# Inverse square roots of a four-layer decoder moved from VectorE's Newton steps to GpSimd powers

## The reference, cut to what matters

```python
def _layernorm(x, axis=-1, eps=1e-05):
    m = jnp.mean(x, axis=axis, keepdims=True)
    v = jnp.var(x, axis=axis, keepdims=True)
    return (x - m) / jnp.sqrt(v + eps)
...
x = x + _L0_attn_ref(_layernorm(x, axis=-1), ...)
x = x + _L0_xattn_ref(_layernorm(x, axis=-1), ...)
...
```

```python
def _l2norm(x):
    return x * jax.lax.rsqrt(jnp.sum(x * x, -1, keepdims=True) + EPS)
```

## Time and profile before

| what | us |
|---|---|
| runs, median (lowest to highest) | 4525.57 (4521.23 to 4525.77) |
| profiled execution, span from first to last instruction | 4502.3 |
| median less the span | 23.3 |
| PE busy | 3949.4 (88%) |
| DVE busy | 2458.5 (55%) |
| ACT busy | 1538.8 (34%) |
| POOL busy | 829.5 (18%) |

### The profile page before, as it was taken

The page is one execution under the profiler, slowest core; times in us unless marked ns, Lnnn a source line. Parts: engine busy times, 40 slices in busy tenths (PEclk is TensorE's granted clock), DMA queues, the critical chain, the costliest instruction groups (busy, mean ns, idle before and its releaser), DMA issues. The chain is left out here.

```text
span 4502.3 us, 98249 instructions
## 1 busy us (share of the span) xinstructions
PE 3949.4 (88%) x39512; PEld 2449.6 (54%) x39512; DVE 2458.5 (55%) x6058; ACT 1538.8 (34%) x3480; POOL 829.5 (18%) x1464
## 2 busy tenths in 40 slices
PE   6998798898799879889879987988987998798898
PEld 4884344465588334446558833444655883344465
DVE  6674534554676453455466745345546765534554
ACT  4452222441454222243144422224314442222431
POOL 2430001130243010112024301011202430101220
PEclk9999999999999999999999999999998999999999
DMA  2001000000000100000000010000000001000000
GB/s 84 3 3 59 8 12 19 24 37 27 27 3 3 59 20 1 19 24 37 27 27 3 3 59 20 1 19 24 37 27 27 3 9 52 20 6 13 24 37 29
DMA packets 11013, 105.17 MB, mean 23 GB/s; under 512 B 1148, under 2 KB 5552, under 8 KB 6192
## 3 DMA queue, kind: packets, MB, share of 16 engines
q1 hardware_dynamic: 10544, 98.69, 5.7%
HBM read 97.64 MB, written 1.05 MB: 22 GB/s over the span
## 5 line engine op out<-in xcount | busy, mean ns | idle before, releaser
L88 PE MATMUL psum<-ident_bf 128*128 128x512 bf16 x2308 | 606.1, 400 | 196.1 <-DVE l_attn_peak L892 58.0
L88 PEld LDWEIGHTS psum<-ident_bf 128*128 128x128 bf16 x2308 | 220.5, 103 | 498.6 <-issue 141.9
L3251 DVE TENSOR_TENSOR l_attn_xx<-l_attn_xx,psum 128x256 f32<-128x256 f32 x512 | 204.4, 418 | 207.4 <-PE psum L2854 195.8
L3016 ACT ACTIVATE l_attn_ax<-psum 128x128 f32<-128x128 f32 (+1 forms) x768 | 185.3, 279 | 361.4 <-PE psum L2835 245.9
L482 DVE TENSOR_TENSOR l_ffn_hidden<-l_ffn_silu,psum 128x512 f32<-128x512 f32 (+2 forms) x176 | 120.9, 687 | 309.4 <-ACT l_ffn_silu L421 309.4
L421 ACT ACTIVATE l_ffn_silu<-psum 128x512 f32<-128x512 f32 (+1 forms) x208 | 124.2, 597 | 460.4 <-PE psum L390 406.8
L94 PEld LDWEIGHTS psum<-streamed_weights,l_ffn_hidden 128*128 128x128 f32 (+1 forms) x1664 | 214.8, 191 | 118.2 <-issue 101.0
L2850 PE MATMUL psum<-l_attn_ax,l_attn_xx 64*64 64x64 f32 x5120 | 267.8, 224 | 0.0
L2854 PE MATMUL psum<-l_attn_xx,l_attn_ax 64*64 64x64 f32 x5120 | 260.5, 221 | 0.0
L3140 POOL TENSOR_TENSOR l_attn_part<-l_attn_ab,streamed_weights 128x128 f32<-128x128 f32 x640 | 246.3, 417 | 39.4 <-PE psum L2835 20.3
L892 DVE TENSOR_REDUCE l_attn_peak<-psum 128x4 f32<-128x2048 f32 (+3 forms) x128 | 185.6, 1487 | 100.1 <-PE psum L789 100.0
(11 more groups left out here) (536 smaller groups left out, 8035.6 us busy)
## 6 DMA issues: line engine op xcount, KB each, us to landing
streamed_weights<-pack_l_ffn SPq DMA_DIRECT2D x4, 5284.0 KB, 16.2
streamed_weights<-pack_l_ffn SPq DMA_DIRECT2D x4, 3972.0 KB, 13.0
streamed_weights<-pack_l_attn SPq DMA_DIRECT2D x5, 2848.5 KB, 9.6
streamed_weights<-pack_l_xattn SPq DMA_DIRECT2D x4, 2496.0 KB, 8.6
streamed_weights<-pack_l_ffn SPq DMA_DIRECT2D x4, 2192.0 KB, 8.4
streamed_weights<-pack_l_xattn SPq DMA_DIRECT2D x4, 2048.0 KB, 8.2
streamed_weights<-pack_l_ffn SPq DMA_DIRECT2D x4, 1923.0 KB, 7.4
streamed_weights<-pack_l_attn SPq DMA_DIRECT2D x4, 1107.5 KB, 4.9
```

Source lines behind the costliest of these rows:

```text
L88: pe.matmul(self.bank(bank), self.ident_bf[:, :], self.ident_bf[:, :].unsqueeze(1).to_broadcast([P, NT, P]), start=True, stop=True)
L3016: act.activation(ax[b, p, :, :], m.psum[b, p, 0:P].rearrange("p (i t) -> p i t", i=2), ACT.Copy).then_inc(ax_ready, 1)
L3251: dve.tensor_tensor(both, both, m.psum[:, p, P:384], ALU.subtract).then_inc(x_less, 1)
```

## The change

`newton_rsqrt` goes from three of its callers. In its place VectorE's epsilon instruction signals GpSimd, GpSimd raises the variances to the power -0.5 (a TENSOR_TENSOR with `ALU.pow` against a column of -0.5 that is set once), and VectorE waits for that before it uses the roots. In the first layer VectorE now goes on to the next convolution chunk and takes the roots up one chunk later. The six warm-up matmuls in each norm that waited for the Newton chain go, and so do the last two groups (seven and four) in the head norm. The other two callers of `newton_rsqrt` stay as they are.

```diff
+        self.minus_half = self.sb("minus_half", [P, 1])
...
+    def root(self, pool, use):
+
+        pool.wait_ge(self.var_ready, use + 1)
+        pool.tensor_tensor(self.rstd[:, :], self.var[:, :], self.m.minus_half[:, :].to_broadcast([P, NT]),
+                           ALU.pow).then_inc(self.rstd_ready, 1)
+
     def statistics(self, dve, chain, src, eps):
...
-        chain.link(dve.tensor_scalar(self.var[:, :], self.mv[:, :, 1], eps, None, ALU.add))
-        newton_rsqrt(dve, chain, self.var[:, :], self.rstd[:, :], self.tmp[:, :])
+        dve.tensor_scalar(self.var[:, :], self.mv[:, :, 1], eps, None, ALU.add).then_inc(self.var_ready, 1)
...
     def tensor(self, pe):
         m = self.m
         m.warm(pe, 9, 2)
-        pe.wait_ge(self.chain, self.base + bool(self.add) + 9)
-        m.warm(pe, 6, 2)
...
     def gpsimd(self, pool):
...
         if self.keep:
             pool.tensor_tensor(m.x[:, :, :], m.x[:, :, :], m.xn[:, :, :], ALU.add).then_inc(self.kept, 1)
+        self.root(pool, self.use)
         if self.bias is not None:
...
     def vector(self, dve):
...
+        dve.wait_ge(self.rstd_ready, self.use + 1)
         for t in range(NT):
             dve.tensor_scalar(m.xn[:, t, :], self.src[:, t, :], self.mv[:, t, 0:1], self.rstd[:, t:t + 1], ALU.subtract,
                               ALU.mult).then_inc(self.xn_ready, 1)
...
(stage_l2_attn)
                 m.norm.gpsimd(pool)
+                pool.wait_ge(var_ready, 1)
+                pool.tensor_tensor(std[:, :, :], var[:, :, :],
+                                   m.minus_half[:, :].unsqueeze(2).to_broadcast([P, 2, NT * H]),
+                                   ALU.pow).then_inc(std_ready, 1)
...
-                for link in (4, 6, 11):
+                for link in (4, 6):
                     pe.wait_ge(chain_sem, link)
                     m.warm(pe, 7, 5)
-                pe.wait_ge(chain_sem, 17)
-                m.warm(pe, 4, 5)
...
-                chain.link(dve.tensor_scalar(var[:, :, :], var[:, :, :], 1.0 / HD, 1e-5, ALU.mult, ALU.add))
-                newton_rsqrt(dve, chain, var[:, :, :], std[:, :, :], tmp[:, :, :])
+                dve.tensor_scalar(var[:, :, :], var[:, :, :], 1.0 / HD, 1e-5, ALU.mult,
+                                  ALU.add).then_inc(var_ready, 1)
+                dve.wait_ge(std_ready, 1)
...
(stage_l0_attn)
                     pool.tensor_tensor(sq[:, i % 2, :], a, a, ALU.mult).then_inc(sq_ready, 1)
+                pool.wait_ge(norm2_ready, 1)
+                pool.tensor_tensor(rs[:, :, :], norm2[:, :, :], m.minus_half[:, :].unsqueeze(2).to_broadcast([P, NT, HV]),
+                                   ALU.pow).then_inc(root_ready, 1)
...
                     if n == NEWTON:
                         dve.wait_ge(sq_psum, 2 * F)
-                        newton_rsqrt(dve, chain, norm2[:, :, :], rs[:, :, :], rs_tmp[:, :, :])
+                        dve.tensor_scalar(norm2[:, :, :], m.psum[:, 6, 0:HV * NT].rearrange("p (t h) -> p t h", h=HV),
+                                          1e-6, None, ALU.add).then_inc(norm2_ready, 1)
+                    if n == NEWTON + 1:
+                        dve.wait_ge(root_ready, 1)
                         dve.tensor_scalar(rs[:, :, 0:2 * F], rs[:, :, 0:2 * F], W ** -0.5, None,
                                           ALU.mult).then_inc(rs_ready, 1)
```

More of the change, by code:

```diff
@@ L133, in __init__ @@
         self.rstd = m.sb("norm_rstd", [P, NT])
-        self.tmp = m.sb("norm_tmp", [P, NT])
         sem = m.pass_sem
         self.chain = sem("norm_chain")
+        self.var_ready = sem("norm_var_ready")
+        self.rstd_ready = sem("norm_rstd_ready")
         self.kept = sem("norm_kept")
@@ L172, in _ @@
                     m.warm(pe, 9, 2)
-                    pe.wait_ge(self.chain, self.links + bool(add) + 9)
-                    m.warm(pe, 6, 2)
                 for half in range(2 if turn else 0):
@@ L184, in _ @@
                     pool.tensor_tensor(m.x[:, :, :], m.x[:, :, :], m.xn[:, :, :], ALU.add).then_inc(self.kept, 1)
+                if norm:
+                    self.root(pool, u)
                 if bias is not None:
@@ L202, in _ @@
                         dve.wait_ge(self.kept, k + 1)
+                    dve.wait_ge(self.rstd_ready, u + 1)
                     for t in range(NT):
@@ L1076, in stage_l2_attn @@
         std = psb("std", [P, 2, NT * H])
-        tmp = psb("tmp", [P, 2, NT * H])
         gain = psb("gain", [P, 2, 4])
@@ L1082, in stage_l2_attn @@
         c_turned = sem("c_turned")
+        var_ready = sem("var_ready")
+        std_ready = sem("std_ready")
         chain_sem = sem("pre_chain")
@@ L2447, in stage_l0_attn @@
         rs = psb("rs", [P, NT, HV])
-        rs_tmp = psb("rs_tmp", [P, NT, HV])
         rsT = psb("rsT", [P, T])
@@ L2460, in stage_l0_attn @@
         rs_ready = sem("rs")
+        norm2_ready = sem("norm2")
+        root_ready = sem("root")
         rs_turned = sem("rs_turned")
@@ L2618, in _ @@
                         dve.wait_ge(sq_psum, 2 * F)
-                        chain.link(dve.tensor_scalar(norm2[:, :, :],
-                                                     m.psum[:, 6, 0:HV * NT].rearrange("p (t h) -> p t h", h=HV),
-                                                     1e-6, None, ALU.add))
-                        newton_rsqrt(dve, chain, norm2[:, :, :], rs[:, :, :], rs_tmp[:, :, :])
+                        dve.tensor_scalar(norm2[:, :, :], m.psum[:, 6, 0:HV * NT].rearrange("p (t h) -> p t h", h=HV),
+                                          1e-6, None, ALU.add).then_inc(norm2_ready, 1)
+                    if n == NEWTON + 1:
+                        dve.wait_ge(root_ready, 1)
                         dve.tensor_scalar(rs[:, :, 0:2 * F], rs[:, :, 0:2 * F], W ** -0.5, None,
@@ L3420, in _ @@
                 dve.tensor_copy(m.later_bf[:, :], m.const["later"])
+                dve.memset(m.minus_half[:, :], -0.5)
         with nc.Fori(0, B) as b:
```

## The result

| | us, median (lowest to highest) | runs |
|---|---|---|
| before | 4525.67 (4521.23 to 4532.70) | 4 |
| after | 4606.38 (4603.51 to 4609.59) | 4 |

The ratio is 1.0185, 95% interval 1.0161 to 1.0208. The forecast was 4460, its range 4410 to 4520.

What follows compares the result with a forecast made beforehand. The prediction took VectorE's Newton chain between variance and normalising, 2.41 us, as the bound in 48 of 52 norms. Terms -89.8 + 7.9 + 7.0 + 9.5 = -65.4 us gave 4460 us, range 4410 to 4520.

Steps and rivals of the forecast that it cites:

- 48 layer norms: Between variance and normalising, a 0.54 us GpSimd round trip replaces 2.41 us of Newton steps: 48 x 1.87 = -89.8 us.
- first norm of each pass: A GpSimd reload ahead of each pass's first power was taken to cost 5.9 us, delaying the norm: 4 x 2.0 = +7.9 us.
- head norm: Second layer's head norm: a 128-column power, 5.6 us with hand-overs, replaces 3.81 us: 4 x 1.75 = +7.0 us.
- query and key norms: First layer's 64-column power of 2.78 us is back before ScalarE takes the turned roots: zero cost.
- GpSimd's work beside normalising: Casts and memsets moved behind the power make VectorE's normalising wait on the shared port: +9.5 us, bounds -3.0 and +17.
- TensorE's clock, warm-ups gone: Behind the norms, removing six warm-ups each was taken not to lower TensorE's clock: zero in the sum.
- the power's price: GpSimd power: 40.6 ns a column over a fixed 181 ns, so 0.34 us for 4 columns and 5.4 for 128.
- Rival 2: Power is dear and the wide norms pay back the gain, losing from 111 ns a column; chance 0.14, 0.10 slower.
- ceiling for the head norm: Upper bound on the head norm's 128-column power: eleven GpSimd products, 4.6 us, losing 4 x 1.0 us.
- Dropping six warm-ups per norm costs nothing by itself: In each norm TensorE then waits 1.3 us or so for the first tile, about the 1.36 it waits now.
- rival 3: TensorE's clock falls behind every norm because six warm-ups are gone: 85 us lost at worst, 4545; chance 0.06.
- three signs: Signs of being wrong: 4-column power over 1 us, 128-column powers over 14, new low-clock stretches behind the norms.

Runs made afterwards that it cites:

- e12: e7 with the head norm's root by a GpSimd power of 128 columns: 4521.6 us, ratio 1.0011.
- e11: e7 with the query and key roots by a GpSimd power over all 64 columns: 4477.4 us, ratio 0.9914.
- e5: e1 with the six warm-up matmuls given back to every norm, started by the variance: 4499.6 us, ratio 0.9964.
- e6: e1 with GpSimd's casts and memsets held back until all four tiles are normalised: 4497.6 us, ratio 0.9950.
- e14: The whole change with the six warm-ups back in every norm, casts and memsets where the change put them: 4607.5 us, ratio 1.0191.
- e1: The change in the 52 layer norms alone; head norm and query and key norms as in the kernel before: 4482.3 us, ratio 0.9918.
- e9: e7 with the query and key roots by a power of 16 columns, a constant for the other 48: 4456.2 us, ratio 0.9872.
- e10: e7 with the query and key roots by a power of 32 columns, a constant for the other 32: 4462.4 us, ratio 0.9887.
- e7: e1 with both the six warm-ups back and GpSimd's casts and memsets held back until the tiles are normalised: 4453.5 us, ratio 0.9866.

## Why the prediction was wrong

| term | forecast | measured |
|---|---|---|
| 48 layer norms | -89.8 | 48 x 1.29 = -61.9 on the path |
| first norm of each pass | +7.9 | 4 x (27.76 - 29.25 + 0.15) = -5.4: the reload is free |
| head norm | +7.0 | 4 x (20.85 - 3.81) = +68.2 (e12: +68.1) |
| query and key norms | 0 | +24 (e11) |
| GpSimd's work beside normalising | +9.5 | 13 - 5 = some +8 |
| TensorE's clock, warm-ups gone | 0 | not measured apart; some 47 of the +81 are left over |

What is left over stands in the first, seventh and ninth sublayers, which are 34, 81 and 21 us longer than in the profile of before and have 46, 107 and 51 us more at 1.2 GHz; of the 34 and 81 the waits explain 28 and 68.

**The step that failed** is the power's price: "I take twice Newton's eleven steps for a logarithm and an exponential, 22 x 1.84 = 40.6 ns a column". It measures 159.6, the work of 87 products, and the fixed part is some 0.4 us and not 0.18 (1014 ns less four columns). Rival 2 was the right mechanism, decided in the place that it named: at 159.6 ns its own formula gives -54.3 + 0.98 x 103.6 = +47 us, 4573. The working had a ceiling for the head norm, eleven products, 4.6 us, although nothing in the trace limits a power from above; a guess of that kind has no upper end, and with 4 x 128 columns on the path it should have weighed the most. From the 4 cycles an element of a dependent chain that the Trainium skill states, page GPSIMD Engine Reference, section 7, the prediction had estimated 73 ns with the same step count; the measurement, 159.6, decides.

**The second step that failed** is "Dropping six warm-ups per norm costs nothing by itself". The argument was that TensorE's wait gets no longer. It does, from 1.36 to 1.64 us; its work between nine warm-ups and the transposes is gone as well, and the clock was at 1.2 GHz at some time in the 8 us behind 48 of 52 norms instead of 19. At the tenth sublayer that took back the whole gain (1.7 us in the projections), and e5 gave it back there (54.7 to 53.5 us). For the kernel as a whole the price stays open: giving the warm-ups back takes 44 us off e6, nothing off the change (e14), and adds 17 to e1 (8 of it in the first norm of each pass). A lower clock behind the norms is rival 3, which had 0.06; it came together with rival 2, which the chances left out. All three signs that the prediction listed as speaking against it were there: a 4-column power over 1 us, a 128-column one over 14, low clock behind the norms.

**A slip in its sums.** At 20 ns a column its own 0.72 us per ns gives 4445, not the 4425 at which its own range begins.

**What held.** The gap of 2.41 us was the right place to read what a root is worth, and the 4-column power lay within the bounds (0.19 to 2.1). The wait on GpSimd's casts came as forecast: 0.69 us more in two expert stages' norms, 0.62 in the last, 1.19 to 1.85 in the ninth sublayer, 13 us in all, less 5 that the epsilon instruction no longer waits. The +1.6 for the first stage's memset didn't come, since normalising took its usual 1.12 us there. The Trainium skill, page SBUF — State Buffer, section "Who interferes with whom", says that a tensor_scalar in its two-port mode and a GpSimd instruction exclude each other; the trace agrees, for memsets too (2.30 us for four tiles). The slack ahead of ScalarE's `rsT` was read rightly ("up to 3.75 us"): 2.90 us is hidden (e9), 5.42 is not (e10).

**The reload** was not on the path. The Trainium skill, page GPSIMD Engine Reference, section 2.1, has about 6 us for a first call; here a power ran 1.6 us behind the reload's entry with its usual 1.01.

**The 23.3 us "around the span"** were not that: the later runs lie 1.7 to 2.2 us above their spans (4608.17 against 4606.4). So the execution profiled of the kernel before took some 4504 us, 21 under its median. That moved neither sign nor sum, since the sum was a difference.

## What to carry to other kernels

Price an instruction that the trace doesn't show by its widest use on the path and leave its upper end open; one short measurement of two widths settles it. Here a GpSimd power beats eleven VectorE steps only up to some 12 columns (0.4 + 12 x 0.16 = 2.3 us and 0.1 of hand-overs, against 2.41), by the path alone; where it is wide it loses. Warm-up matmuls that hang on a chain of steps go with the chain: when the chain is shortened, hang them on what remains, and move other GpSimd work out from between its result and the VectorE instruction that waits. Here the two had to be done together, and where the warm-ups ran at 0.43 us each they were too many.

## What the runs showed of the hardware

- A GpSimd power on 128 partitions took 1.01, 2.90, 5.42, 10.53 and 20.74 us for 4, 16, 32, 64 and 128 columns: a straight line of 157 to 160 ns a column over some 0.4 us.
- TensorE's clock can differ far behind an edit. In the ninth sublayer a stretch some 115 us behind the norm ran at 0.53 in e5 and at 0.81 in e7, and its four passes took 617 us in e5, 621 in e6 and 584 in e7, one execution each. Two edits that cost 17 and 15 us singly by the medians (on e1) gain 29 together.
- The same sublayer of the unchanged kernel took 144.7 to 150.6 us in the four passes of one execution, the longest with 27 us at 1.2 GHz and the others with 14. Runs of the unchanged kernel spread from 4502.8 to 4536.1 us (4503.1 at a mean granted clock of 0.965, 4536.1 at 0.956). A small gain is better judged at its own stage first, and only then by the kernel's time.
